# Routed experts: gate and up products in three passes of high and low parts, weights split per tile

## The reference

```
h = _rms(x, w_ln2).reshape(B * S, H)                       # 2048 rows of 512
logits = h @ w_router                                      # 8 experts
top_w, top_i = jax.lax.top_k(softmax(logits), 2)
g = einsum('th,ehi->eti', h, w_gate_e)                     # 512 -> 352, each expert
u = einsum('th,ehi->eti', h, w_up_e)
y = einsum('eti,eih->eth', silu(g) * u, w_down_e)          # 352 -> 512
routed = einsum('eth,te->th', y, combine)                  # the two chosen experts
sh = silu(h @ w_sh_gate) * (h @ w_sh_up) @ w_sh_down       # shared expert, 512 -> 1408 -> 512
x = x + routed + sh * sigmoid(h @ w_sh_eg)
```

## Time and profile before

| | |
|---|---|
| runs | 2178.59, 2180.32, 2185.15 us |
| profiled execution, span from first to last instruction | 2186.9 us |
| PE busy | 2027.6 us (93%) |
| VectorE, ScalarE, POOL busy | 1212.3, 895.1, 698.4 us |
| routed experts, gate and up (L1935) | 624 instructions, 195.3 us |
| routed experts, down (L1954) | 234 instructions, 107.0 us |
| clock granted to TensorE, mean | 0.962 of full speed |

### The profile page before, as it was taken

The page is one execution under the profiler, slowest core; times in us unless marked ns, Lnnn a source line. Parts: engine busy times, 40 slices in busy tenths (PEclk is TensorE's granted clock), DMA queues, the critical chain, the costliest instruction groups (busy, mean ns, idle before and its releaser), DMA issues. The chain is left out here.

```text
span 2186.9 us, 31487 instructions
## 1 busy us (share of the span) xinstructions
PE 2027.6 (93%) x10679; PEld 1359.5 (62%) x10679; DVE 1212.3 (55%) x2649; ACT 895.1 (41%) x1695; POOL 698.4 (32%) x610
## 2 busy tenths in 40 slices
PE   7997999978799999997998999979999998999998
PEld 6875666666433334334776666658878887565564
DVE  6454666467799898876776666554323153122221
ACT  3424555345377676773542544534212211111111
POOL 0003655346423132323564655511000000232332
PEclk9997999989899999998998899989999999999999
DMA  5638576356754545453567666453112055233331
GB/s 197 221 142 180 140 166 149 104 181 251 252 148 114 149 107 151 102 126 122 191 219 202 155 157 153 121 184 137 49 48 77 1 202 221 42 61 61 66 60 36
DMA packets 150834, 297.67 MB, mean 136 GB/s; under 512 B 24594, under 2 KB 43156, under 8 KB 149588
## 3 DMA queue, kind: packets, MB, share of 16 engines
q1 hardware_dynamic: 112900, 242.29, 37.7%
q10 hardware_dynamic: 29040, 34.74, 5.9%
q0 software_dynamic: 8736, 18.62, 4.6%
HBM read 181.55 MB, written 102.50 MB: 130 GB/s over the span
## 5 line engine op out<-in xcount | busy, mean ns | idle before, releaser
L1339 ACT ACTIVATE cross_c_prob<-bank 128x512 f32<-128x512 f32 x512 | 271.2, 598 | 115.1 <-PE bank L1192 113.5
L1389 DVE TENSOR_REDUCE row_max<-bank 128x2 f32<-128x1024 f32 x248 | 290.6, 1212 | 25.9 <-PE bank L1158 24.9
L1847 PE MATMUL bank<-moe_hT,moe_w 128*128 128x512 f32 x1056 | 250.7, 393 | 7.6 <-DVE moe_w L2090 7.6
L1192 PE MATMUL bank<-stack 56*128 56x512 f32 (+4 forms) x768 | 231.4, 426 | 6.7 <-ACT cross_c_prob L1339 3.1
L1847 PEld LDWEIGHTS bank<-moe_hT,moe_w 128*128 128x128 f32 x1056 | 199.4, 190 | 50.2 <-issue 7.8
L1158 PE MATMUL bank<-stack 48*128 48x512 f32 (+4 forms) x720 | 189.9, 442 | 25.9 <-PEq L71 13.5
L1192 PEld LDWEIGHTS bank<-stack 56*128 56x128 f32 (+1 forms) x768 | 117.9, 192 | 134.7 <-ACT cross_c_prob L1339 69.2
L1935 PE MATMUL bank<-moe_w_e,moe_hT_e 128*128 x624 | 195.3, 466 | 5.5 <-DMA moe_w_e<-in_experts_packed 5.1
L1935 PEld LDWEIGHTS bank<-moe_w_e,moe_hT_e 128*128 128x128 f32 x624 | 116.6, 192 | 67.7 <-issue 9.5
L1339 ACT ACTIVATE rotary_c_prob<-bank 128x512 f32<-128x512 f32 (+3 forms) x256 | 106.1, 437 | 124.8 <-PE bank L1195 121.4
L1339 ACT ACTIVATE first_c_prob<-bank 128x512 f32<-128x512 f32 (+3 forms) x256 | 105.9, 436 | 123.4 <-PE bank L1195 120.7
(11 more groups left out here) (391 smaller groups left out, 4070.9 us busy)
## 6 DMA issues: line engine op xcount, KB each, us to landing
moe_w_e<-in_experts_packed SPq DMA_DIRECT2D x8, 2176.0 KB, 9.0
qk_parts<-first_p_parts SPq DMA_DIRECT2D x32, 512.0 KB, 2.6
stack<-qk_parts SPq DMA_DIRECT2D x64, 256.0 KB, 6.7
qk_parts<-cross_p_parts SPq DMA_DIRECT2D x32, 512.0 KB, 2.6
stack<-qk_parts SPq DMA_DIRECT2D x256, 64.0 KB, 2.6
qk_parts<-rotary_p_parts SPq DMA_DIRECT2D x32, 512.0 KB, 2.8
moe_raw<-in_shared_packed SPq DMA_DIRECT2D x11, 768.0 KB, 8.4
stack<-qk_parts SPq DMA_DIRECT2D x16, 512.0 KB, 5.6
```

Of the source, the lines that this page charges most:

```text
L1192: last = nc.tensor.matmul(bank[:, 0 : S - q0], k_stack[slot][r : r + ALL_ROWS, at, m * P : (m + 1) * P], q_stack[slot][r : r + ALL_ROWS, a ...
L1339: nc.scalar.activation(probability(g, step // HEADS_AT_ONCE, step % HEADS_AT_ONCE), psum[bank_at["score", n]][:, 0 : S - q0], ACT.Exp).the ...
L1389: nc.vector.tensor_reduce(row_max[:, g % 2, m, j - 1 : j + 1], c.banks[:, first : first + WIDE, :], AX_X, ALU.max).then_inc(s.max_done, 1)
L1847: last = nc.tensor.matmul(psum[bank][:], weights(pa, f, k), hT[p % 2][:, pb, k, :], start=m == 0, stop=m == len(steps) - 1)
```

## The change

The gate and up products of the routed experts become three passes of high and low parts. The stationary rows are split as they leave the transpose: ScalarE writes the high part (`columns_high`), VectorE the low part (`columns_low`). The moving weights are split for each tile anew from the fp32 weights in SBUF: they are cut along the contraction into 4 chunks of 704 columns (352 gate, 352 up), ScalarE rounds `w_ln` times a chunk (`chunk_high`), VectorE makes `w_ln` times the chunk minus the rounded one (`chunk_low`). Each of the 4 chunks has one buffer, so a chunk of tile t+1 is made after PE has used that of tile t (`e_chunk`). A tile's gate and up are 24 matmuls of 352 columns, chunk by chunk, with a wait ahead of each chunk. `w_ln` moves from the rows to the weights. The packed weights become two arrays, gate and up (8 loads) and down (8 loads, after the former); the first chunk waits for the gate and up loads, the first down product for the down loads. `owner[t]` is read by ScalarE and VectorE too, and by PE ahead of the down product. On VectorE the copies of tile t-1 now stand at the start of round t. `chunk0` lies over arrays that the routing no longer needs, `chunks12` in what was padding, chunk 3 in the shared expert's `inner`. The down product is as before.

```diff
 def gate_up(t):                                   # PE
-    e = pe.value_load(owner[0:1, t : t + 1], min_val=0, max_val=E - 1)
-    experts[t] = e
-    pe.wait_ge(s.e_hT, t + 1)
-    if t == 0:
-        pe.wait_ge(s.e_weights, 16 * E)
+    pe.wait_ge(s.e_hT_lo, t + 1)
     if t == 1:
         pe.wait_ge(s.s_out, TT * B)
     if t >= 2:
         pe.wait_ge(s.e_inner, t - 1)
-    for half in range(2):
-        for k in range(KD):
-            rhs = w_gu_e[:, bass.ds(e, 1), k, half * FE : (half + 1) * FE].rearrange("p a n -> p (a n)")
-            last = nc.tensor.matmul(psum[1 + 2 * (t % 2) + half][:, 0:FE], hT_e[:, t % 2, k, :], rhs, start=k == 0, stop=k == KD - 1)
-    last.then_inc(s.e_gate_up, 1)
+    for k in range(KD):
+        pe.wait_ge(s.e_w_lo, KD * t + k + 1)
+        for half in range(2):
+            for pa, pb in ((0, 0), (0, 1), (1, 0)):
+                last = nc.tensor.matmul(psum[1 + 2 * (t % 2) + half][:, 0:FE], hT_e[:, t % 2, pa, k, :], w_chunk[k][:, pb, half * FE : (half + 1) * FE],
+                                        start=k == 0 and (pa, pb) == (0, 0), stop=k == KD - 1 and (pa, pb) == (1, 0))
+        last.then_inc(s.e_chunk, 1)
...
 def down_e(t):                                    # PE, after its two waits for innerT
+    if t == 0:
+        pe.wait_ge(s.e_down_here, 16 * E)
...
+    e = pe.value_load(owner[0:1, t : t + 1], min_val=0, max_val=E - 1)
...
+def columns_high(t):                              # ScalarE
+    act.wait_ge(s.e_turned, t + 1)
+    if t >= 2:
+        act.wait_ge(s.e_chunk, KD * (t - 1))
+    nc.scalar.activation(hT_e[:, t % 2, 0], psum[X][:].rearrange("p (k n) -> p k n", k=KD), ACT.Copy).then_inc(s.e_hT_hi, 1)
+def chunk_high(t, k, e):
+    if t:
+        act.wait_ge(s.e_chunk, KD * (t - 1) + k + 1)
+    elif k:
+        act.wait_ge(s.s_down, N_F)
+    src = gate_up_e[:, bass.ds(e, 1), k * CHUNK : (k + 1) * CHUNK].rearrange("p a n -> p (a n)")
+    nc.scalar.activation(w_chunk[k][:, 0], src, ACT.Copy, scale=w_ln[:, k : k + 1]).then_inc(s.e_w_hi, 1)
...
 act.wait_ge(s.m_owners, 4)
+act.wait_ge(s.e_gate_up_here, 16 * E)
+e = owner_of(0)
+chunk_high(0, 0, e)
+columns_high(0)
+for k in range(1, KD):
+    chunk_high(0, k, e)
 for t in range(PER):
-    act.wait_ge(s.e_gate_up, t + 1)
+    if t + 1 < PER:
+        e = owner_of(t + 1)
+        columns_high(t + 1)
+        for k in range(KD - 1):
+            chunk_high(t + 1, k, e)
+    act.wait_ge(s.e_chunk, KD * (t + 1))
     if t >= 2:
         act.wait_ge(s.e_inner, t - 1)
     nc.scalar.activation(silu_e[:, t % 2], psum[1 + 2 * (t % 2)][:, 0:FE], ACT.Silu).then_inc(s.e_silu, 1)
+    if t + 1 < PER:
+        chunk_high(t + 1, KD - 1, e)
     if t:
         result(t - 1)
...
-def columns(t):                                   # VectorE
...
+def columns_low(t):
+    dve.wait_ge(s.e_hT_hi, t + 1)
+    nc.vector.tensor_tensor(hT_e[:, t % 2, 1], psum[X][:].rearrange("p (k n) -> p k n", k=KD),
+                            hT_e[:, t % 2, 0].bitcast(F32), ALU.subtract).then_inc(s.e_hT_lo, 1)
+def chunk_low(t, k, e):
+    dve.wait_ge(s.e_w_hi, KD * t + k + 1)
+    src = gate_up_e[:, bass.ds(e, 1), k * CHUNK : (k + 1) * CHUNK].rearrange("p a n -> p (a n)")
+    nc.vector.scalar_tensor_tensor(w_chunk[k][:, 1], src, w_ln[:, k : k + 1], w_chunk[k][:, 0].bitcast(F32),
+                                   ALU.mult, ALU.subtract).then_inc(s.e_w_lo, 1)
...
+dve.wait_ge(s.m_owners, 4)
+e = owner_of(0)
+chunk_low(0, 0, e)
+columns_low(0)
+for k in range(1, KD):
+    chunk_low(0, k, e)
 evacuate(LAST)
 for t in range(PER):
+    if t:
+        turned_inner(t - 1)                       # the two copies, L2264 and L2266
+    if t + 1 < PER:
+        e = owner_of(t + 1)
+        columns_low(t + 1)
+        for k in range(KD - 1):
+            chunk_low(t + 1, k, e)
     dve.wait_ge(s.e_silu, t + 1)
     if t >= 2:
         dve.wait_ge(s.e_inner_turned, t - 1)
     nc.vector.tensor_tensor(inner_e[:, t % 2], silu_e[:, t % 2], psum[2 + 2 * (t % 2)][:, 0:FE], ALU.mult).then_inc(s.e_inner, 1)
+    if t + 1 < PER:
+        chunk_low(t + 1, KD - 1, e)
+turned_inner(PER - 1)
...
-last_f_of = lambda e: min(KF - 1, max(0, ((e + 1) * EXPERT_W * 4 - 1 - 2 * KD * S * 4) // (2 * SHARED_W * 4)))
+last_f_under = lambda end: min(KF - 1, max(0, (4 * end - 1 - 2 * KD * S * 4) // (2 * SHARED_W * 4)))
...
 for e in range(E):                                # SyncE
-    sp.wait_ge(s.s_down, LAST * KF + last_f_of(e) + 1)
-    sp.dma_start(w_e[:, e], a.experts[e]).then_inc(s.e_weights, 16)
+    sp.wait_ge(s.s_down, LAST * KF + last_f_under((e + 1) * GATE_UP_W) + 1)
+    sp.dma_start(gate_up_e[:, e], a.experts_gate_up[e]).then_inc(s.e_gate_up_here, 16)
+for e in range(E):
+    sp.wait_ge(s.s_down, LAST * KF + last_f_under(E * GATE_UP_W + (e + 1) * DOWN_W) + 1)
+    sp.dma_start(down_w_e[:, e], a.experts_down[e]).then_inc(s.e_down_here, 16)
```

More of the change, by code:

```diff
@@ L1633 @@
 SHARED_W = 2 * KD * P + D
-EXPERT_W = KD * 2 * FE + len(FE_K) * D
+GATE_UP_W, DOWN_W = KD * 2 * FE, len(FE_K) * D
+CHUNK = 2 * FE
 RAW_WEIGHTS = [f"w_raw{f}" for f in range(KF)]
@@ L1643 @@
     "s_gate", "s_up", "s_silu", "s_inner", "s_inner_hi", "s_inner_lo", "s_down", "s_x2", "s_x3", "s_residual", "s_out", "s_stored",
-    "e_weights", "e_row0", "e_row1", "e_row2", "e_row3", "e_turned", "e_hT", "e_gate_up", "e_silu", "e_inner", "e_inner_turned",
+    "e_gate_up_here", "e_down_here", "e_row0", "e_row1", "e_row2", "e_row3", "e_turned", "e_hT_hi", "e_hT_lo", "e_w_hi", "e_w_lo", "e_chunk", "e_silu", "e_inner", "e_inner_turned",
     "e_innerT01", "e_innerT", "e_down", "e_result", "e_added",
@@ L1689, in moe_phase @@
             rt, squares = sb1("rt", [n_col, S]), sb1("squares", [P, D])
+        with ExitStack() as after_routing:
+            chunk0 = after_routing.enter_context(nc.sbuf_tensor("moe_chunk0", [P, 2, CHUNK], F32R))
         nmax, ex, total = sb("nmax", [P, NT]), sb("ex", [P, NT, E]), sb("total", [P, NT])
@@ L1711, in moe_phase @@
             raw = [sb3(f"raw{f}", [P, 2, SHARED_W]) for f in range(KF)]
-        w_e = sb("w_e", [P, E, EXPERT_W])
-        sb("w_pad", [P, SHARED_W * 2])
-        hT_e, silu_e, inner_e = sb("hT_e", [P, 2, KD, P]), sb("silu_e", [P, 2, FE]), sb("inner_e", [P, 2, FE])
+        gate_up_e, down_w_e = sb("gate_up_e", [P, E, GATE_UP_W]), sb("down_w_e", [P, E, DOWN_W])
+        chunks12 = sb("chunks12", [P, 2, 2, CHUNK], F32R)
+        sb("w_pad", [P, SHARED_W * 2 - 4 * CHUNK])
+        hT_e, silu_e, inner_e = sb("hT_e", [P, 2, 2, KD, P], F32R), sb("silu_e", [P, 2, FE]), sb("inner_e", [P, 2, FE])
         innerT = sb("innerT", [P, 2, len(FE_K), P])
+        chunk3 = inner[:].rearrange("p a b n -> p (a b n)")[:, 0 : 2 * CHUNK].rearrange("p (a n) -> p a n", a=2)
+        w_chunk = (chunk0[:], chunks12[:, 0], chunks12[:, 1], chunk3)
         row, y = xt, res
@@ L1720, in moe_phase @@
         w_d = lambda part, f: w[f][:, part, 2 * KD * P : SHARED_W]
-        w_gu_e = w_e[:, :, 0 : KD * 2 * FE].rearrange("p e (k n) -> p e k n", k=KD)
-        w_dn_e = w_e[:, :, KD * 2 * FE : EXPERT_W].rearrange("p e (k n) -> p e k n", k=len(FE_K))
+        w_dn_e = down_w_e[:].rearrange("p e (k n) -> p e k n", k=len(FE_K))
         rows = lambda m, b: m[b * S : (b + 1) * S, :].rearrange("(t p) d -> p t d", p=P)
-        last_f_of = lambda e: min(KF - 1, max(0, ((e + 1) * EXPERT_W * 4 - 1 - 2 * KD * S * 4) // (2 * SHARED_W * 4)))
+        last_f_under = lambda end: min(KF - 1, max(0, (4 * end - 1 - 2 * KD * S * 4) // (2 * SHARED_W * 4)))
         with nc.Block() as block:
@@ L1770, in _ @@
                 sp.wait_ge(s.m_rows_stored, 16 * B)
-                sp.wait_ge(s.e_weights, 16 * E)
+                sp.wait_ge(s.e_gate_up_here, 16 * E)
+                sp.wait_ge(s.e_down_here, 16 * E)
             @block.gpsimd
@@ L1910, in _ @@
                 down(N_F - 1)
-                experts = {}
                 def front(t):
@@ L1916, in front @@
                     if t >= 1:
-                        pe.wait_ge(s.e_hT, t)
+                        pe.wait_ge(s.e_hT_lo, t)
                     for k in range(KD):
@@ L1949, in down_e @@
                     pe.wait_ge(s.e_innerT01, t + 1)
+                    if t == 0:
+                        pe.wait_ge(s.e_down_here, 16 * E)
                     if t >= 2:
                         pe.wait_ge(s.e_result, t - 1)
+                    e = pe.value_load(owner[0:1, t : t + 1], min_val=0, max_val=E - 1)
                     for n, (k0, kn) in enumerate(FE_K):
-                        rhs = w_dn_e[0:kn, bass.ds(experts[t], 1), n, :].rearrange("p a n -> p (a n)")
+                        rhs = w_dn_e[0:kn, bass.ds(e, 1), n, :].rearrange("p a n -> p (a n)")
                         last = nc.tensor.matmul(psum[6 + t % 2][:], innerT[0:kn, t % 2, n, :], rhs, start=n == 0, stop=n == len(FE_K) - 1)
@@ L2043, in result, with owner_of @@
                     nc.scalar.activation(y[:, t % 2, :], psum[6 + t % 2][:], ACT.Copy, scale=slot_w[:, t : t + 1]).then_inc(s.e_result, 1)
```

(39 more changed lines are left out.)

## The result

2153.83 us median of 4 runs (2151.03 to 2159.80) beside 2179.45 for the kernel before (4 runs, 2170.80 to 2185.15). The ratio is 0.9894, interval 0.9865 to 0.9922. That is 23 us less by the ratio (17 to 29 by its interval); forecast were 24, a time of 2156 and a range of 2145 to 2173.

The account below looks back on a forecast made before the run. PE was taken to bound the kernel, the gather loop just under it. 19 us from 36 shorter rounds plus 5.2 at the start made 24: 2180.3 - 24 = 2156 us, range 2145 to 2173.

Parts of the forecast that it names:

- PE bounds before, the loop lies just under it: Routed experts before the change: two PE rounds take 16.16 us, the gather path 15.99, so PE just wins.
- the loop: Routed experts: tile t+4's gather follows tile t's scatter, which needs its down product; two rounds hold this path plus one PE round.
- 24 matmuls 0.16 apart, 3.85 us: Gate and up on PE: 24 matmuls of 352 columns take 3.85 us per tile (3.53 to 4.32), replacing 4.74.
- The loop binds at 7.55, with 0.10 on top 7.65: Round after the change: 7.55 us against PE's 7.19, plus the 0.10 by which earlier rounds exceeded their floor; saves 19 us.
- The terms 3.61, 4.2, 0.1 and 7.19: Two rounds: down product's end to gather start 3.61 us, landing 4.2, landing to first transpose 0.1, one PE round 7.19.
- Splits: Chunk rounding on ScalarE 0.84 us, subtraction on VectorE 0.93; 5.1 and 5.6 us per tile, both fitting beside PE.
- The start, 5.2 us: Start of the routed experts: gate and up weights load earlier, so gate_up(2) starts about 5.2 us earlier than before.
- this risk: Start of the routed experts: if the clock falls in PE's gaps too, up to 2 us of the gain are lost.
- Rival A: VectorE holds up POOL's indirect DMAs by one chunk_low, 0.9 us per round: 8 us saved, 2172; chance 0.17.
- Rival C: Gathers land sooner when POOL is earlier, so PE binds at 7.29 us a round: 37 us saved, 2143; chance 0.12.
- Each microsecond costs half: Routed experts' rounds: if a cover were gone, each microsecond of result delay would cost half a microsecond per round.
- B: VectorE holds up both scatter and gather issues, descriptors land late: 9 us slower with two full chunk_low, 2189; chance 0.05.

Follow-up runs that it names:

- gather-first edit: The kernel before, with the gather of tile t+4 issued ahead of the scatter of tile t instead of behind it: 2171.97 us, ratio 0.9981.
- runs with two passes: The changed kernel without the low rows by high weights pass: 2132.68 us; the same with tile t+4's gather ahead of tile t's scatter: 2092.85 us.
- gather-first version: The changed kernel with the gather of tile t+4 issued ahead of the scatter of tile t instead of behind it: 2138.93 us, ratio 0.9829.

## Why the prediction was right

1. *PE bounds before, the loop lies just under it.* Right. Without the loop, rounds are 8.07 before and 7.19 after. The second is the forecast PE round, 7.19. One reading was loose: the 32 in the earlier trace rows are weight loads that waited, of the 35 gathers in that stretch; PE itself stood for 5.
2. *24 matmuls 0.16 apart, 3.85 us.* Right: 3.86.
3. *The loop binds at 7.55, with 0.10 on top 7.65.* Right: 7.69. The path is the forecast one; the size was right in part by luck. The terms 3.61, 4.2, 0.1 and 7.19 give 15.10 for two rounds, and 15.37 were measured. Of these 0.27, the landing is the whole: PE stood for 24 of the 35 gathers from tile 4 on, and those landed 4.48 after their start on average, where the forecast took the median of before, 4.2. The other terms came to 10.89 for 10.90. What covered the gap was the 0.10 a round carried over from before. There it was late gathers too: the gather-first edit takes it away, and PE stood for 5 of 35, which landed after 4.60. But nothing in the forecast said that they would cost about as much when PE stands for 24 as when it stands for 5, 0.14 a round against 0.11. Saved were 17.7 us, not 19.
4. *Splits.* 0.84 and 0.93 were forecast, 0.886 and 0.952 measured. They fit as forecast, and by the runs with two passes they would fit in a round of 5.9.
5. *The start, 5.2 us.* 4.7. After its front(0), gate_up(0) came at 2.5, as forecast, and gate_up(1) at 11.7, forecast 12.2. But gate_up(1) took 4.82 where 3.86 is usual (the chain below), because the granted clock stood at half (the 1.2 GHz level) for part of it, after PE had stood 1.6 us ahead of front(2) and 2.3 us ahead of turn(0) behind evacuate and the chunks: the forecast had named this risk and not priced it in.

```profile
1850.25 1.41 DVE moe_res L2149 x2
...
1853.11 1.73 DVE moe_chunks L2293 x2
...
1856.22 4.82 PE bank L1939 x24
```

The window over it, with a mean clock of 0.79, that is 3.4 of 8 us at half:

```profile
1854.00:1862.00 8.00, 6.68 (x30) 6.12 (x31) 6.11 (x9) 3.56 (x5) 0.00 (x0) 0.79 0.18 66
```

6. *Rival A, VectorE holds up POOL.* The mechanism is real, the price was too high. An issue that starts inside a chunk_low stands until that is over, but it starts late in it: 0.3 is lost instead of 0.9, on half of the gathers, and at most 0.09 a round. The forecast's own sign for A, gather issues over 1.0, did come. The Trainium skill ("SBUF — State Buffer", Who interferes with whom) makes two-SBUF-input VectorE work a lock on GpSimd instructions that read SBUF, and infers that descriptor generation is spared. By the gathers' ends the lock holds for them too; the inference does not fit these runs. Whether the gather stands over its read of the row numbers or over its descriptors, they do not show.
7. *Rival C, the gathers keep up.* Wrong for this kernel, but it is the time of the gather-first version: 2143 forecast, 2139 measured.
8. *"Each microsecond costs half."* Right for what PE has in the loop (1.29 shorter gave 0.64 a round), wrong between scatter and gather, where only 0.4 of a delay reaches the landing. The forecast took 4.2 as the landing's own time. The sum used no delay there, so it did not suffer; the prices of rivals A and B did, for they let a delay of the gather into the loop in full.

## What to carry to other kernels

When PE is full, also look for the longest loop that returns to it through another engine and a DMA, over as many rounds as there are buffers. It costs next to nothing until PE gets faster. Here the shorter products brought 18 us in the rounds with the loop in place, and would have brought 32 without it (36 x 0.88, gather-first against gather-first). And look whether the order of a queue, not the data, puts a transfer into that loop: here one gather moved ahead of one scatter gave the rest back. Of the landings put the mean of those that PE will stand for into such a sum, not the median of all.

## What the hardware did that I had not expected

- An indirect gather's issue on POOL takes 0.99 alone. When it starts inside a VectorE instruction with two SBUF inputs, it ends 0.86 after that instruction's end, wherever in it the gather began (all 17 in the kernel after, 0.25 to 0.71 in): 1.27 when 0.41 of the instruction were left, 1.57 when 0.70 were. If POOL starts first, nothing is added, with up to 0.9 us of overlap.
- A gather of 128 rows lands 3.4 us after its start when the scatter ahead of it was issued 3.4 earlier, or when there was none (3.3), and 4.3 when it was 1.9 earlier.
- What comes ahead of the routed experts differs by up to 15 us from one profile to another (front(0) from 1836 to 1851), by 10.5 between two kernels whose code ahead of it is the same (1850.58 before, 1840.03 with the gather first). A difference of spans has to be cut by stage before it is explained.
